# The mixer's products within heads laid out by place in a tile, on four diagonal tiles of the array

## The reference, cut to what matters

```python
q = silu(conv(x @ Wq, conv_q_w)); k = ...; v = ...        # causal depthwise convolution, 4 taps
gk = -exp(A_log) * softplus(x @ Wgk + dt_bias)            # decay, per token and head
beta = sigmoid(x @ Wb + bb)
q = _rope(_l2norm(q), DK // 2); k = _rope(_l2norm(k), DK // 2)   # 16 heads of 32 channels
def step(S, ins):                                         # over the 128 tokens, state 32 x 32 per head
    S = S * exp(g_t); pred = k_t @ S
    delta = b_t * (v_t - pred)
    S = S + outer(k_t, delta)
    return S, q_t @ S
o = o * rsqrt(mean(o * o) + EPS) * gnorm_w * silu(x @ Wg); return o @ Wo
```

## Time and profile before

| What | us |
|---|---|
| median of 3 runs (lowest, highest) | 1478.54 (1475.56, 1484.55) |
| the profiled execution, time | 1479.14 |
| its span in the profile | 1477.3 |
| mean granted TensorE clock, share of full speed | 0.945 |
| mixer in the trace, norm to L1266 | 586.2 to 730.5 |

### The profile page before, as it was taken

One profiled execution on the slowest core, in us unless ns is written; L12 is line 12 of the kernel. 1 busy time (PEld: TensorE's weight loads), 2 busy tenths in 40 slices (PEclk: granted clock), 3 DMA queues, 4 the chain that ended last, 5 costly groups with the idle time before them and its releaser, 6 DMA issues.

```text
span 1477.3 us, 22537 instructions
## 1 busy us (share of the span) xinstructions
PE 1365.1 (92%) x9326; PEld 1140.6 (77%) x9326; DVE 916.1 (62%) x1190; ACT 617.3 (42%) x749; POOL 22.0 (1%) x26
## 2 busy tenths in 40 slices
PE   7999999999999997869869999999894869999998
PEld 6888888788888885638557777777653539999997
DVE  5666565665556556694449888888615386544444
ACT  4323333423323222530337777777501234555442
POOL 0000000000000000200000000000100000000000
PEclk9999999999999999885679999999997889999999
DMA  7101001300000031100128998999840124545542
GB/s 262 37 15 36 16 29 43 114 16 29 15 30 15 15 115 57 58 29 2 58 99 332 342 342 340 344 340 344 331 181 7 57 86 155 185 173 185 185 174 96
DMA packets 35462, 195.46 MB, mean 132 GB/s; under 512 B 3504, under 2 KB 3760, under 8 KB 15664
## 3 DMA queue, kind: packets, MB, share of 16 engines
q1 hardware_dynamic: 33040, 185.29, 34.2%
q0 software_dynamic: 2336, 8.91, 1.8%
HBM read 193.67 MB, written 0.52 MB: 131 GB/s over the span
## 4 chain that ended last, share of the span: by engine, by line
PE 85%; DVE 10%; issue 2%; DMA 2%; ACT 2%; POOL 0%; DVEq 0%; SPq 0%; POOLq 0%; ACTq 0%
PE psum L441 13%; PE psum L1995 12%; PE psum L389 12%; PE psum L1430 7%; PE psum L1450 4%; PE psum L1433 4%; PE psum L418 4%; PE psum L480 3%; PE psum L466 3%; PE psum L1977 3%; PE psum L900 2%; PE psum L1453 2%; PE psum L2008 1%; PE psum L1827 1%; PE psum L1462 1%
## 5 line engine op out<-in xcount | busy, mean ns | idle before, releaser
L389 PE MATMUL psum<-arena_r 128*128 128x512 f32 x768 | 241.5, 453 | 7.4 <-ACT arena_r L699 7.4
L1491 DVE TENSOR_TENSOR arena_r<-ring,arena_r 128x2048 fp32r<-128x2048 f32 x96 | 219.6, 2289 | 38.9 <-ACT arena_r L1485 38.7
L441 PEld LDWEIGHTS psum<-ring_r,arena_r 128*128 128x128 f32 x1536 | 186.0, 192 | 6.1 <-issue 5.7
L1485 ACT CAST arena_r<-ring 128x2048 fp32r<-128x2048 f32 x96 | 183.4, 1912 | 16.5 <-PE psum L1433 11.2
L441 PE MATMUL psum<-ring_r,arena_r 128*128 128x256 f32 x1536 | 189.4, 285 | 0.0
L1995 PE MATMUL psum<-arena_r 128*128 128x256 f32 x1536 | 184.5, 283 | 1.1 <-DVE arena_r L2054 1.1
L1995 PEld LDWEIGHTS psum<-arena_r 128*128 128x128 f32 x1536 | 184.4, 192 | 1.2 <-issue 1.2
L389 PEld LDWEIGHTS psum<-arena_r 128*128 128x128 f32 x768 | 140.9, 190 | 54.3 <-issue 8.7
L1950 DVE TENSOR_TENSOR arena_r<-ring,arena_r 128x2048 fp32r<-128x2048 f32 x44 | 100.8, 2292 | 117.0 <-ACT arena_r L1945 117.0
L418 PE MATMUL psum<-cst,arena 128*128 128x128 f32 x512 | 133.8, 271 | 0.5 <-DVE arena L581 0.5
L1430 PE MATMUL psum<-arena_r 128*128 128x512 f32 x512 | 132.5, 401 | 1.3 <-issue 1.3
(11 more groups left out here) (295 smaller groups left out, 1739.3 us busy)
## 6 DMA issues: line engine op xcount, KB each, us to landing
ring<-in_stream SPq DMA_DIRECT2D x151, 1024.0 KB, 4.8
arena<-in_ctxT POOLq DMA_DIRECT2D x8, 1024.0 KB, 11.1
arena<-in_ctxT SPq DMA_DIRECT2D x7, 1024.0 KB, 9.2
arena<-in_wk SPq DMA_DIRECT2D x16, 256.0 KB, 2.7
wv_in<-in_wv SPq DMA_DIRECT2D x8, 512.0 KB, 3.4
arena<-in_wq SPq DMA_DIRECT2D x16, 256.0 KB, 2.6
arena<-in_wo SPq DMA_DIRECT2D x2, 1024.0 KB, 6.3
row<-in_rows SPq DMA_DIRECT2D x1, 1320.0 KB, 14.6
```

The source lines that it names most:

```text
L389: last = nc.tensor.matmul(bank, wk_sb[wp][:, c, :], cx[xp][kb][:, c, :], start=c == wp == xp == 0, stop=c == C - 1 and xp == 1)
L441: last = nc.tensor.matmul(bank[:, q * T:(q + 1) * T], cx[xp][kc // 4][:, c, kc % 4 * P:(kc % 4 + 1) * P], wv_sb[wp][:, c, :], start=c == w ...
L1485: nc.scalar.copy(mwhi[p % MB], ring[k % RING][:, :]).then_inc(moe_hi, 1)
L1491: nc.vector.tensor_tensor(mwlo[p % MB], ring[(BLK_MOE + p) % RING][:, :], mwhi[p % MB].bitcast(fp32), ALU.subtract).then_inc(moe_lo if p < ...
```

## The change: what it does

Token tiles, not tokens, become the layout. A partition now stands for (head's place in its chunk, token within its tile of 32), and everything else (chunk, batch, tile) lies along the free axis. Head i of a chunk then has rows 32i to 32i+31 as input and as output, which is the array tile on the diagonal.

- Decays: masks from constants (`fold`, `upto`, `after`, `own`, `between`) replace POOL's `gm`, `gmc` and the eight groups over 128 x 128. Within tiles: `decd`, 8 fp32 products of 128x128x128 and 2 one-pass ones. Across tiles: `deco`, for each of 8 (chunk, batch) pairs two products with 192 moving columns (three tiles against all later tokens: 96 + 64 + 32). ACT makes `wide_g`, the decay repeated 32 times.
- `tile_products` (k.k and k.q within tiles, 128 products each) and `later_products` (across, 96 each, of 96, 64 and 32 columns) replace L963 and `head_products`. The four row groups write the same bank, each its own 32 partitions.
- `beta` and `nk` are put into the new order by PE (`place`) and copied by DVE (`placed_dve`).
- v is transposed in 32x32 blocks by DVE inside `vp_dve`; PE's transposes L979 go.
- `earlier`, `within` and `outputs` use tile (i, i) for head i. `rest_dve` and `solved_dve` become 128x128 operations. The output product is split by token tile, accumulating in PSUM, and follows two tiles behind.
- Order: v's convolution goes into the inverse (levels 29 and 25), q's to levels 17 and 14, rope to 10 and 8, `vp_dve` to 19, `um_dve` behind the inverse. On PE the gate's projection stands before the cross-tile products, as one run.
- Constants grow from 1920 to 2336 columns, 208 KB.

```diff
@@ mixer_pool
-            gp.wait_ge(g_ready, 1)
-            for g in range(G8):
-                nc.gpsimd.tensor_tensor(four(gm, g), per_row(C_("le"), 4), per_elem(by_head(gdec[:, :, :])[:, 4 * g:4 * g + 4], P),
-                                        ALU.mult).then_inc(gm_ready, 1)
@@ new helpers
+        def tile_products(right, bank):
+            for g in range(G):
+                for a in range(NT):
+                    for i in range(4):
+                        r, t = tile_rows(i), tile_rows(a)
+                        o = g % 4 * P + a * DK
+                        last = nc.tensor.matmul(psum[r, bank + g // 4, o:o + DK], krot[r, g // B, g % B, t],
+                                                right[r, g // B, g % B, t], start=True, stop=True)
+            return last
+        def later_products(right):
+            for g in range(G):
+                for a in range(NT - 1):
+                    for i in range(4):
+                        r = tile_rows(i)
+                        o = g % 2 * LATER + LATER_AT[a]
+                        n = P - (a + 1) * DK
+                        last = nc.tensor.matmul(psum[r, g // 2, o:o + n], krot[r, g // B, g % B, tile_rows(a)],
+                                                right[r, g // B, g % B, P - n:], start=True, stop=True)
+            return last
+        def place(v, bank):
+            for a in range(NT):
+                for i in range(4):
+                    last = nc.tensor.matmul(psum[tile_rows(i), bank, a * G:(a + 1) * G], C_("ident")[:, tile_rows(a)],
+                                            v.rearrange("p (b c i) -> p i c b", b=B, i=4)[:, i, :, :], start=True, stop=True)
+            return last
@@ mixer_pe, from the k projection on
+            for k in range(2):
+                nc.tensor.matmul(psum[:, k, :], fold_r[0:DK, :], past_r[0:DK, :].unsqueeze(1).to_broadcast([DK, 4, P]),
+                                 start=True, stop=False)
+                for g in range(4 * k, 4 * k + 4):
+                    h = g % B * H + 4 * (g // B)
+                    last = nc.tensor.matmul(psum[:, k, g % 4 * P:g % 4 * P + P], later_g[:, h:h + 4, :], C_("upto"),
+                                            start=False, stop=g % 4 == 3)
+            last.then_inc(decd_filled, 1)
+            for c in range(C):
+                project_mix(pe, 1, 0, c)
             turn_mix(pe, 0, 4)
...
+            for c in range(C):
+                project_mix(pe, 1, 1, c)
+            pe.wait_ge(beta_ready, 1)
+            place(beta[:, :], 2).then_inc(placed, 1)
+            pe.wait_ge(rope_ready, 1)
+            tile_products(krot, 4).then_inc(kkd_filled, 1)
+            pe.wait_ge(nk_ready, 1)
+            place(nk[:, :], 3).then_inc(placed, 1)
...
+            for g in range(G):
+                b, h = g % B, 4 * (g // B)
+                out = psum[:, g // 2, g % 2 * LATER:(g % 2 + 1) * LATER]
+                nc.tensor.matmul(out, later_g[:, b * H + h:b * H + h + 4, :], C_("own", LATER), start=True, stop=False)
+                last = nc.tensor.matmul(out, wide_g[:, b * H + h:b * H + h + 4, :], C_("between", LATER),
+                                        start=False, stop=True)
+                if g % 2:
+                    last.then_inc(deco_filled, 1)
+            turn_mix(pe, 2, 6)
             pe.wait_ge(uc_ready, 1)
+            for cc in range(C):
+                for c in range(C):
+                    project_mix(pe, 3, cc, c)
+            pe.wait_ge(deco_exp, 4)
+            later_products(krot).then_inc(kk_filled, 1)
@@ the solve
             def within(a, b):
-                for h in range(H):
-                    last = nc.tensor.matmul(psum[tile_rows(a), b, h * DK:(h + 1) * DK], xt[tile_rows(a), :, b * H + h],
-                                            right[tile_rows(a), b, h * DK:(h + 1) * DK], start=True, stop=True)
+                for cc in range(C):
+                    for i in range(4):
+                        r = tile_rows(i)
+                        last = nc.tensor.matmul(psum[r, 6 + b, cc * DK:(cc + 1) * DK], xt[r, :, (cc * B + b) * NT + a],
+                                                rhs[r, b, cc, :] if a else vp[r, cc, b, 0, :], start=True, stop=True)
...
+            pe.wait_ge(xt_ready, 1)
+            pe.wait_ge(rope_ready, 2)
+            for b in range(B):
+                within(0, b)
+            pe.wait_ge(mix_gs, 2)
+            tile_products(qrot, 4).then_inc(qk_filled, 1)
+            for a in range(1, NT):
+                for b in range(B):
+                    earlier(a, b)
+                if a == 1:
+                    later_products(qrot).then_inc(qk_filled, 1)
+                for b in range(B):
+                    within(a, b)
+                if a == 2:
+                    pe.wait_ge(pm_ready, 2)
+                if a >= 2:
+                    for b in range(B):
+                        outputs(a - 2, b)
...
+            for b in range(B):
+                outputs(NT - 2, b)
+            for b in range(B):
                 pe.wait_ge(x_ready, B * (NT - 1) + b + 1)
+                outputs(NT - 1, b).then_inc(o_filled, 1)
@@ mixer_act
             square_mix_act(act, 0, 0)
+            act.wait_ge(decd_filled, 1)
+            nc.scalar.activation(decd, psum[:, 0:2, :].rearrange("p k (n r) -> p (k n) r", r=DK), ACT.Exp, scale=-1.0).then_inc(decd_exp, 1)
+            nc.scalar.copy(wide_g, per_elem(by_head(gdec[:, :, :]), DK)).then_inc(wide_ready, 1)
...
+                evac_mix_act(act, 1, cc)
+            silu_mix_act(act, 1)
+            for cc in range(C):
                 evac_mix_act(act, 2, cc)
+            for k in range(4):
+                act.wait_ge(deco_filled, k + 1)
+                nc.scalar.activation(deco[:, 2 * k:2 * k + 2, :], psum[:, k, 0:2 * LATER].rearrange("p (g t) -> p g t", g=2),
+                                     ACT.Exp, scale=-1.0).then_inc(deco_exp, 1)
+            silu_mix_act(act, 2)
@@ mixer_dve
+            nc.vector.tensor_tensor(beta[:, :], beta[:, :], by_head(bnum[:, :, :]), ALU.mult).then_inc(beta_ready, 1)
+            placed_dve(dve, 0, betap[:, :])
+            link(dve, nc.vector.tensor_tensor(decb, decd, per_elem(betap[:, :], DK), ALU.mult))
+            dve.wait_ge(kkd_filled, 1)
+            nc.vector.tensor_tensor(ucol.rearrange("p r m -> p m r"), psum[:, 4:6, :].rearrange("p k (n r) -> p (k n) r", r=DK),
+                                    decb, ALU.mult).then_inc(uc_ready, 1)
...
+            placed_dve(dve, 1, nkp[:, :])
             for r in range(DK - 1, 0, -1):
                 inverse_level_dve(dve, r)
-                if r == 28 or r == 24:
-                    conv_mix_dve(dve, 2, r == 24)
-                if r == 13:
+                if r == 29 or r == 25:
+                    conv_mix_dve(dve, 1, r == 25)
+                if r == 19:
                     vp_dve(dve)
-                if r == 12:
+                if r == 17 or r == 14:
+                    conv_mix_dve(dve, 2, r == 14)
+                if r == 10:
                     rope_start_dve(dve, 2, qrot)
-                if r == 9:
+                if r == 8:
                     rope_dve(dve, 1, qrot, 6)
-                if r == 5:
-                    um_dve(dve, 0)
...
-            um_dve(dve, 1)
+            um_dve(dve)
```

More of the change, by code:

```diff
@@ L57 @@
 NEXP = 3 * FQ
[L60 to L64, removed]
+CONST_NAMES = ["ident", "le", "gt", "past", "fold", "upto", "after", "own", "between", "ropec", "ropes",
+               "partner", "iota", "sums", "heads0", "heads1", "heads2", "heads3"]
+CONST_WIDTH = {"after": DK, "own": P + P // 2, "between": P + P // 2}
+CONST, NCONST = {}, 0
+for const_name in CONST_NAMES:
+    CONST[const_name] = NCONST
+    NCONST += CONST_WIDTH.get(const_name, P)
 FAR = 1000.0
-NCONST = P * len(CONST_NAMES)
 ROWS = {"x0_bo": (0, D), "x0_gamma": (D, D), "x0_beta": (2 * D, D), "mix_dt": (3 * D, H),
@@ L87, in constants @@
     r, c = np.indices((P, P))
-    t = {"ident": r == c, "le": r <= c, "gt": r > c, "gt32": (r > c) & (r // DK == c // DK), "past": (r > c) * FAR}
-    t["mixed"] = np.where(c < DK, r % DK <= c, (c < 2 * DK) * (r % DK >= c % DK) * FAR)
+    t = {"ident": r == c, "le": r <= c, "gt": r > c}
+    t["past"] = (r < DK) * (r > c % DK) * FAR
+    t["fold"] = (r < DK) * (r == c % DK)
+    t["after"] = (c < DK) * (r % DK > c)
+    t["upto"] = (r // DK == c // DK) * (r <= c)
+    tile, token = np.array([(a, t) for a in range(P // DK) for t in range((a + 1) * DK, P)]).T
+    for n, v in (("own", r[:, :1] // DK == tile), ("between", (r[:, :1] // DK > tile) & (r[:, :1] <= token))):
+        t[n] = v
     of_head = c % H == 4 * (c // H % C) + r // DK
@@ L805, in build @@
         nk = sb("nk", [P, BH])
+        betap = sb("betap", [P, M])
+        nkp = sb("nkp", [P, M])
         gcol = sb("gcol", [P, DK])
@@ new lines, in within, with outputs @@
+                last.then_inc(u_filled, 1)
+            def outputs(a, b):
+                for cc in range(C):
```

(20 more changed lines are left out.)

215 lines of the change are left out of this document (75 added, 140 removed).

## The result

The changed kernel takes 1472.6 us in the median of 8 runs (1469.25 to 1475.39), the one before 1481.24 in 8 runs beside it: ratio 0.9945, 95% interval 0.9922 to 0.9967. By the ratio that is 8.1 us or 0.55% faster, where 1.09% was forecast. The time lies inside the forecast range and on the figure given for the rival "program supply sets (c)", 1472. The profiled execution took 1474.05, 5.1 less than the profiled one of before. Of these 5.1 us the mixer gives 3.0 (141.3 instead of 144.3); it also starts 1.0 earlier, and what follows it is 1.1 shorter.

What follows compares the result with a forecast made beforehand. It took DVE and PE in turns, then DVE alone in the inverse, then PE to bound the mixer. 17.7 - 1.5 = 16.2 off 1479.1 gave 1462.9; the runs' median, 0.6 lower, 1462.5; range 1451 to 1478.

Steps and rivals of the forecast that it cites:

- program supply sets (c): Rival: in the solve after the inverse, PE stops 0.9 at each of 11 instruction packets, 10 instead of 1.4; 1472; chance 0.14.
- program supply: Term for PE waiting for its instructions in the solve: 11 packets, one each 2.8 us, adding 1.4 us.
- stretch (c): The solve after the inverse, where PE sets the time: 47.8 us before, 32.0 forecast, bounds 22 and 40.
- signs named in advance: Signs of a wrong forecast: diagonal products over 20 ns each, L900 at 0.45 after 653, or inverse ending later than PE.
- 1.5 more was forecast: Behind the solve: same work, but less runs before it to raise the clock, +1.5 us, bounds 0 and +5.5.
- POOL's removal, -3.6: At k's convolution on DVE: without POOL's decay products the convolutions are no longer slowed and end at 607.3, -3.6 us.
- To the inverse, -2.7: From k's convolution to the inverse's start: 14.9 us instead of 17.6, with one stop counted 0.9, -2.7 us.
- the inverse, +3.0: DVE's inverse, 37.1 us before: gains v's half convolutions and transpose, loses L1152 and a wait for ACT, +3.0 us.
- PE was to be 1.5 late: At the inverse's end: PE finishes the cross-tile products at 663.8, 1.5 us late, taking that end from DVE.
- the overlap: In the solve: four diagonal tiles run at once, so 32 columns cost 14 ns at half clock instead of 57.
- The rival in which the tiles don't overlap: Every product on diagonal tiles runs one at a time: solve 111 instead of 32, about 1565 us; chance 0.11.
- full clock in (c): Rival: in the solve, dense tiles keep the clock the gate's projections raised, 22 instead of 32; 1452.5 us; chance 0.13.

Runs made afterwards that it cites:

- e11: The changed kernel with POOL's eight 128x512 operations put back on scratch that nothing reads; ratio to before 1.0013 in 12 runs.
- e12: The kernel before with one of POOL's eight operations left, its result used for all eight groups; ratio 0.9974 in 12 runs.
- e2: The changed kernel with as many MATMULs, but twice the columns for most of q's diagonal products and `within`; 1474.69 us in one execution.
- e5: The changed kernel with the 1 MB transfer of the experts' third block held until the mixer's last outputs; ratio to before 0.9949 in 10 runs.
- e6: The changed kernel with q projected before v and its 448 small MATMULs issued beside the inverse; ratio to before 0.9891 in 4 runs.
- e7: The kernel of e6, also with the experts' third block held as in e5; ratio to before 0.9892 in 4 runs.
- e4: The same kernel as e5, the changed one with the experts' third block held, in its first single execution; 1464.02 us.
- e3: The same kernel as e11, the changed one with POOL's eight operations put back, in one execution; 1478.73 us.

## Why the prediction was wrong, and what of it held

- **The step that failed is the term "program supply" of stretch (c): "I add 1.4".** It measured 16.3 us of stops in the profile of the changed kernel (13.4 in e11's, with as many instructions in the solve). The forecast had 11 packets at one each 2.8 us, and took that to be near a turn with a stop. A turn is 3.5 to 4.0 us for 128 MATMULs, and 1536 MATMULs in 30.6 us are one such block each 2.5; so there is a stop at almost every block. It also priced a stop by its own length instead of by the turn that it ends. The rival priced it at 0.9, half of the only one in the trace, and even its 10 us was low. Of the signs named in advance, this one came: diagonal products slower than forecast, with gaps marked issue.
- **That the rival's total, 1472, met the measured time is luck.** The solve was 8.4 us longer than the rival had it, and the stretches around it were better than forecast. `within` starts 2.2 us early, 1.0 of it because the whole mixer starts 1.0 earlier in this profile. From the squares' start to the residual add it took 15.8 us; before it took 17.0, and 1.5 more was forecast. Six of the ten other profiles of versions of the changed kernel have that part, counted from the squares' end, as long as before (16.4 us; 14.7 here), so this gain is not the change's own.
- **POOL's removal, -3.6: right in its place.** The convolutions ended at 605.97, forecast 607.3. e12 agrees with the price in the kernel before: 3.8 us (1.6 to 6.1), where 3.1 is its share of the 3.6. In the changed kernel the ratios with and without POOL's operations, 1.0013 and 0.9945, lie 0.0068 or 10 us apart; by their two intervals that is anything from 6 to 14. There the rotation or a projection loses its clock as well. The forecast had the full-clock rotation in the next step; the profiles show it as a consequence of this one.
- **To the inverse, -2.7; the inverse, +3.0: right.** The inverse takes 40.2 us, 3.1 more than before. The stops before it were 2.18 and 2.12, not one of 0.9; of these only the first lies on the way to it. The chain passes from the gate's projection to the cross-tile products, as forecast, but PE and DVE arrive within 0.2 us of each other, where PE was to be 1.5 late.
- **Stretch (c): the overlap was right.** At half clock 128 MATMULs of L934 take 1.93 us. With the last one's 0.24 off that is 13 ns each, where 14 was forecast; one tile alone took 57. The 16.3 us of stops taken off the solve's 49.0 leave 32.7; forecast for the MATMULs and waits was 30.6. The rival in which the tiles don't overlap is out.
- **The clock:** most of the solve ran at the 0.50 level, as the sum took it. The rival "full clock in (c)" could not have gained its 10 us: at 1.00 a turn still took 3.45 us (e2), and at 0.87 still 3.73 (e5), as the stop grew by what the MATMULs lost.
- **Where the expected gain went.** The solve lost its serial chains and got a queue of instructions in exchange. It has 2.5 times as many MATMULs (1552 for 623) at a quarter of the time each, and 12 turns of 3.8 us are 46 of its 50 us. What the two parts of the change are worth depends on the order in which they are counted. With POOL's work in both kernels the new layout gives nothing (1.0013). With seven eighths of it gone from the kernel before (0.9974), the changed kernel's 0.9945 leaves the layout some 4 us, and their intervals overlap. The layout pays clearly only when the k.q products leave the solve (e6).

The Trainium skill, TensorEngine Tiling (Array Packing), "Gotcha 1: PSUM Pressure", by which row tiles can't access one bank at once, does not hold for these tiles: the four of one head group write one bank, each its own 32 partitions, and 13 ns per MATMUL is a quarter of the 57 of one tile.

The DMA view of the changed kernel, 660 to 712 us in 40 slices of 1.3 us:
```profile
GB/s 107 397 321 0 0 13 0 0 13 0 0 13 0 0 13 0 0 13 0 0 13 0 0 13 0 0 13 0 0 13 0 0 13 0 0 13 0 0 0 13
...
q8 instruction: 13, 0.21, 1.8%
```
and of the kernel before:
```profile
GB/s 0 0 0 0 0 13 0 0 0 0 0 0 13 0 0 0 0 0 0 13 0 0 0 0 0 0 0 13 0 0 0 0 0 0 0 13 0 0 120 359
...
q8 instruction: 5, 0.08, 0.6%
```
Each 13 is one fetch of 16 KB. Before, one in 9 to 10 us, as the work needs it; after, one in every third slice without a gap. The fetches and the turns go together. In the solves of the changed kernel and its versions other than e6 and e7 (nine profiles), PE resumes 83 times after a stop; the next fetch starts 1.0 to 1.8 us later (middle value 1.13), and PE resumes again, where there is a stop, 2.2 to 3.0 us after a fetch has started (2.42). The packet itself takes only 0.9 to 1.5 us. That reads as a round trip, one fetch behind the other, and not as a queue short of bandwidth; why no second fetch is under way meanwhile, no run shows. The kernel before held the price already: beside L963 its fetches start at 621.9 and 625.5, 3.6 us apart, and the 1.59 us of MATMULs and the stop of 1.76 in the earlier trace rows add up to 3.4. The Trainium skill, Runtime: NRT & Kernel Launch, "Instruction fetch mechanics", gives a refill as 16 KiB or 256 instructions. The traces agree: 0.21 MB in 13 packets is 16 KB, and 128 MATMULs with their LDWEIGHTS are 256. The same section calls the refill mostly hidden; here it is not, as 256 of these instructions run in 1.9 us and a refill comes every 3.7.

## What to carry to other kernels

Count instructions, not only columns. Tiles side by side make each MATMUL cheap, but once PE runs a block of 128 MATMULs in less than some 3.7 us, the supply of instructions sets the time. A stretch of many small products is then worth splitting, with a part of it moved beside work of another engine (e6).

A single stop marked "issue" amid fast MATMULs is a sample of a rate. Add it to the time that the block before it took: that sum is the turn, and every further block costs about as much, however fast it runs (3.5 to 4.0 us here).

And repeat a promising single execution before building on it: e4's promised 10 us, and ten runs gave none.

## What the runs showed of the hardware that was not expected

- PE is fed in blocks of 128 MATMULs with their LDWEIGHTS. In nine profiles with a dense solve (all of the changed kernel and its versions but e6 and e7) the starts of two fetches lie 3.3 to 4.5 us apart (89 intervals, middle value 3.73). The stops came after 127 or 128 MATMULs, or twice that where a block had come in time.
- Little runs ahead. Before the solve PE spent 7 us on the gate's 32 MATMULs, and the trace has no fetch from 651 to 663 us. Yet the first stop came after only 243 further MATMULs, not quite two blocks.
- A 1 MB transfer beside a fetch made that one stop 3.2 to 3.9 us (seven profiles) instead of 0.86 and 1.35 (e4, e5).
- POOL's 128x512 operations slow DVE's three-operand ones beside them: twelve convolutions took 9.15 us in e3 (472 to 1256 ns each), against 476 to 485 ns each in the changed kernel. Through PE's idle time of 3.0 to 3.5 us they also took the granted clock from the work behind (0.59 and 0.55 in e3 and e11, 1.00 without them).
